# Decoder block on one core: the first attention group's score and maxima units in a new order, its maxima row sent by ScalarE, and two group loads issued at other places

## The reference, cut to what matters

```python
Q = (x @ Wq.T + bq).reshape(b, s, H, hd)      # K, V alike
scores = (gt * scores_cross + (1.0 - gt) * scores_conv) * hd ** -0.5
scores = jnp.where(causal, scores, -jnp.inf)
attn = jax.nn.softmax(scores, axis=-1)
out = jnp.einsum('bhqk,bkhd->bqhd', attn, V)
```

## Time and profile before

| | before |
|---|---|
| median of 3 runs | 1066.88 us |
| the runs | 1066.5, 1066.88, 1082.13 us |
| the profiled execution, its own time | 1068.4 us |
| its span, first to last instruction | 1066.7 us |
| mean granted TensorE clock | 0.985 of full |
| PE busy | 1024.2 us |
| DVE busy | 720.5 us |
| ACT busy | 576.9 us |

### The profile page before, as it was taken

The page is one execution under the profiler, slowest core; times in us unless marked ns, Lnnn a source line. Parts: engine busy times, 40 slices in busy tenths (PEclk is TensorE's granted clock), DMA queues, the critical chain, the costliest instruction groups (busy, mean ns, idle before and its releaser), DMA issues.

```text
span 1066.7 us, 19123 instructions
## 1 busy us (share of the span) xinstructions
PE 1024.2 (96%) x7108; PEld 604.0 (57%) x7108; DVE 720.5 (68%) x1603; ACT 576.9 (54%) x1093; POOL 198.3 (19%) x220
## 2 busy tenths in 40 slices
PE   4999899999999999999999999899999999999998
PEld 3877344444444444444444465444544588888887
DVE  6878887877787787878785386556566355555552
ACT  3776276767676676767676667376466411111110
POOL 6655000000000000000000034111001033333331
PEclk9999799999999999999999999899999999999999
DMA  8596904444433344444401046688663100000001
GB/s 259 189 269 222 192 2 81 82 82 82 82 62 57 65 72 81 86 85 82 81 13 20 11 122 159 141 157 155 124 118 62 31 8 21 20 21 20 20 21 40
DMA packets 82186, 93.27 MB, mean 87 GB/s; under 512 B 14660, under 2 KB 75296, under 8 KB 80557
## 3 DMA queue, kind: packets, MB, share of 16 engines
q1 hardware_dynamic: 79579, 88.87, 38.2%
q10 hardware_dynamic: 2514, 3.18, 1.4%
HBM read 53.55 MB, written 28.80 MB: 77 GB/s over the span
## 4 chain that ended last, share of the span: by engine, by line
PE 78%; DVE 12%; ACT 3%; issue 2%; DMA 2%; SPq 1%; POOL 0%; POOLq 0%; DVEq 0%; ACTq 0%
PE bank L134 20%; PE bank L837 12%; PE bank L870 12%; PE bank L856 10%; DVE pm L767 5%; PE bank L1503 3%; PE bank L1128 3%; PE bank L860 3%; PE bank L842 2%; PE bank L1395 2%; PE bank L1405 2%; PE bank L968 2%; PE bank L1397 2%; PE bank L1380 2%; PE bank L1382 1%
## 5 line engine op out<-in xcount | busy, mean ns | idle before, releaser
L767 DVE TENSOR_REDUCE pm<-bank 128x1 f32<-128x512 f32 (+3 forms) x608 | 356.5, 652 | 86.4 <-PE bank L842 69.7
L814 ACT ACTIVATE prob<-bank 128x512 f32<-128x512 f32 (+1 forms) x608 | 317.4, 584 | 172.0 <-PE bank L860 86.8
L837 PE MATMUL bank<-stk,stq 96*128 96x512 bf16 (+3 forms) x768 | 223.5, 334 | 5.5 <-DVE pm L767 3.4
L856 PE MATMUL bank<-stq,stk 98*128 98x512 bf16 (+3 forms) x768 | 221.0, 328 | 1.7 <-DMA stq<-mrow 0.8
L837 PEld LDWEIGHTS bank<-stk,stq 96*128 96x128 bf16 x768 | 67.9, 97 | 134.2 <-DVE pm L767 76.9
L870 PE MATMUL bank<-prob,va 128*17 128x512 f32 (+3 forms) x1536 | 143.8, 492 | 0.0
L1630 ACT ACTIVATE e_sg<-bank 128x512 f32<-128x512 f32 x48 | 28.7, 598 | 177.0 <-PE bank L134 174.9
L1349 ACT ACTIVATE xprob<-bank 80x512 f32<-80x512 f32 x128 | 72.8, 593 | 71.7 <-PE bank L1397 68.8
L753 POOL TENSOR_TENSOR xres<-xres,bo_b 128x256 f32<-128x256 f32 x32 | 23.2, 724 | 398.5 <-DVE pm L767 204.1
L856 PEld LDWEIGHTS bank<-stq,stk 98*128 98x128 bf16 x768 | 69.1, 98 | 45.4 <-ACT prob L814 9.1
L842 PE MATMUL bank<-tri_q,identb 128*128 128x128 bf16 (+2 forms) x352 | 87.0, 247 | 0.0
(11 more groups left out here) (183 smaller groups left out, 1347.1 us busy)
## 6 DMA issues: line engine op xcount, KB each, us to landing
qk<-a_parts SPq DMA_DIRECT2D x32, 384.0 KB, 2.7
xq<-c_parts SPq DMA_DIRECT2D x16, 384.0 KB, 3.1
xstq<-xq SPq DMA_DIRECT2D x32, 192.0 KB, 4.3
stq<-qk SPq DMA_DIRECT2D x30, 192.0 KB, 3.9
stk<-qk SPq DMA_DIRECT2D x15, 384.0 KB, 6.3
vs<-a_vst SPq DMA_DIRECT2D x8, 544.0 KB, 3.8
oall<-u_out SPq DMA_DIRECT2D x64, 64.0 KB
xstq<-xq SPq DMA_DIRECT2D x32, 128.0 KB, 4.7
```

The source lines that it names most:

```text
L767: nc.vector.tensor_reduce(pm[:, k, h0:h0 + hb, r], src[:, 0:hb * w].rearrange("p (h w) -> p h w", h=hb), AX, ALU.max).then_inc(s_mxe, 1)
L814: nc.scalar.activation(prob[:, U % NPS, 0:hb * n], bank[STB[U % NSB]][:, 0:hb * n], ACT.Exp).then_inc(s_ex, 1)
L837: mm = nc.tensor.matmul(dst[:, h * w:(h + 1) * w], stq[i][0:R, half, h0 + h, r * P:(r + 1) * P], stk[i][0:R, h0 + h, k0:k0 + w], start=(h ...
L856: mm = nc.tensor.matmul(dst[:, h * n:(h + 1) * n], stk[i][0:RM, h0 + h, kt * P:(kt + 1) * P], stq[i][0:RM, half, h0 + h, q0:q0 + n], start ...
```

## The change

- Group 0 gets an order of its own (`first_plan`). Ahead of the barrier TensorE does ring places 11 to 15 only (`LEAD` = 16) instead of 11 to 38. After it come places 16 to 19, then the first half's 11 score units with the other 19 places among them (one or two with each), then, behind unit 10, the second half's transpose and the first 6 maxima units of group 1, and then the 27 score units of the second half with the other 33 maxima units of group 1 among them. The other groups keep `plan`. VectorE's code doesn't change its order, but `self_vector(v, range(N_AHEAD, NMX - 1))` stays as it is: it goes through places 11 to 38 as they come, and waits for the barrier after them.
- ACT arrives at the barrier, then waits for the first half's row of group 0 and sends it (`send_maxima(a, 0, 0)`), then waits for the barrier. SP sent it before, after the barrier.
- SP issues group 1's load behind chunk 5's stores, ahead of those of chunks 6 and 7.
- SP issues group 2's load, behind group 0's second maxima row. ACT did so before.

```diff
--- before.py
+++ after.py
@@ -271,7 +271,8 @@
 
             for c in range(NCH):
                 chunk(c)
-            load_self(sp, 1)
+                if c == 5:
+                    load_self(sp, 1)
             for u in range(2):
                 sp.wait_ge(so[u], 64 * B)
                 sp.wait_ge(vo[u], 16 * B)
@@ -659,6 +660,29 @@
             plan += [("r", n, 1) for n in range(at, upto)]
             at = upto
 
+        LEAD = n_half + 5
+
+        def first_plan():
+
+
+            own = [("r", n, 0) for n in range(LEAD, NMX - 1)]
+            order, own = own[:4], own[4:]
+            ahead = [("r", n, 1) for n in range(NMX - 1)]
+            for u in range(NST):
+                order.append(("s", u, 0))
+                order += [("p", s, 0) for s in range(len(sets)) if joint_end[s] - 1 == u - LAG]
+                if u < half_end[0]:
+                    upto = len(own) * (u + 1) // half_end[0] - len(own) * u // half_end[0]
+                    at = len(own) * u // half_end[0]
+                    order += own[at:at + upto]
+                if u == half_end[0] - 1:
+                    order += [("r", NMX - 1, 0)] + ahead[:6]
+                    ahead = ahead[6:]
+                if u >= half_end[0]:
+                    w, n = u - half_end[0], NST - half_end[0]
+                    order += ahead[len(ahead) * w // n:len(ahead) * (w + 1) // n]
+            return order
+
         side[0] = "right"
         stq, stk, va = [], [], []
 
@@ -710,11 +734,14 @@
                               .rearrange("c (r h) s -> (c r) h s", h=HP)[:, heads]).then_inc(ld[n], 16)
             eng.dma_start(va[n][:].rearrange("p n d h -> p n (d h)"), vs[g]).then_inc(ld[n], 16)
 
+        def send_maxima(eng, g, c):
+            eng.wait_ge(s_mxe, g * NMX + ring.index(("t", c)) + 1)
+            eng.dma_start(stq[g % NB][R:RM, c].rearrange("a h q -> a (h q)"),
+                          mrow[:, g % 2, c]).then_inc(md[g % 2][c], 16)
+
         def self_sync(sp):
             def maxima(g, c):
-                sp.wait_ge(s_mxe, g * NMX + ring.index(("t", c)) + 1)
-                sp.dma_start(stq[g % NB][R:RM, c].rearrange("a h q -> a (h q)"),
-                             mrow[:, g % 2, c]).then_inc(md[g % 2][c], 16)
+                send_maxima(sp, g, c)
 
             def store(g):
 
@@ -728,9 +755,11 @@
                 sp.dma_start(den[rows * i:rows * (i + 1), b],
                              u_out[HD:P:VW, g % 2].rearrange("a (c t) -> a c t", t=DT)).then_inc(us[g % 2], 16)
 
-            maxima(0, 0)
             for g in range(G):
                 maxima(g, 1)
+                if g == 0:
+                    for i in range(2, NB):
+                        load_self(sp, i)
                 if g:
                     store(g - 1)
                     if g + NB - 1 < G:
@@ -804,8 +833,6 @@
                 nc.scalar.activation(u_out[:, g % 2, c * 512:(c + 1) * 512], bank[PVB[c]][:],
                                      ACT.Identity).then_inc(s_u, 1)
 
-            for i in range(2, NB):
-                load_self(a, i)
             for g in range(G):
                 for u, (half, kt, h0, hb, q0, n, diag) in enumerate(st_units):
                     U = g * NST + u
@@ -880,7 +907,7 @@
             t.wait_ge(s_r, 4 * NCH)
             t.wait_ge(s_ve, 2 * NCH)
             for g in range(G):
-                for what, which, ahead in plan:
+                for what, which, ahead in plan if g else first_plan():
                     if g == G - 1 and what == "s" and which in EARLY:
                         if which == min(EARLY):
                             t.wait_ge(s_mxe, G * NMX)
@@ -1829,7 +1856,9 @@
             @block.scalar
             def _(a):
                 qkv_scalar(a)
-                barrier(a, 1)
+                arrive(a)
+                send_maxima(a, 0, 0)
+                a.wait_ge(s_phase, 5)
                 self_scalar(a)
                 mid_scalar(a)
                 barrier(a, 2)
@@ -1841,7 +1870,7 @@
             def _(t):
                 qkv_tensor(t)
                 arrive(t)
-                self_tensor(t, range(N_AHEAD, NMX - 1))
+                self_tensor(t, range(N_AHEAD, LEAD))
                 t.wait_ge(s_phase, 5)
                 self_tensor(t, None)
                 mid_tensor(t)
```

## The result

The changed kernel's median is 1073.59 us over 20 runs, that of the kernel before 1068.55 us over 20, runs that are added to the three shown above. The ratio is 1.0062, with a 95% interval of 1.0042 to 1.0082: 4.5 to 8.8 us slower, within 2%. The ratio leaves out executions over 1.5% above the fastest of their kernel; the two medians alone lie 5.0 us apart. The forecast was 1068.9 us, 2.0 us slower than before, with a range up to 1072.2.

A forecast was written before the change was run, and what follows sets the result against it. It took TensorE to bound the kernel and VectorE's reductions to pace the passage between the stages. +1.4 (to the second half) and +0.6 (second half) made +2.0 on 1066.9, so 1068.9 us; range 1065.3 to 1072.2.

The forecast's parts named there:

- What bounds the passage: From 109 us until group 0 is through: scores beside maxima help only as far as VectorE does not stop.
- VectorE's slack: From 109 us to group 1's first score: 38 us of reductions in 45.6 us, some 7 us of slack.
- When the barrier opens: End of stage one: last value store lands after 6.2 us behind the moved load, barrier opens at 115.2, as today.
- faster: Rival at the barrier: store lands at 112.3, barrier opens at 112.4; total 1065.9 us, chance 17%.
- VectorE's stop: Behind the first transpose, at the barrier: VectorE loses 4.8 us, eight reductions, from 111.6 to 116.4.
- To the second half's first score: From the barrier to that score: VectorE sets the pace, score at 134.5 against 133.09, +1.4 us.
- VectorE's starving: In group 0's 23 reductions behind the barrier: 0.7 us, bounds 0.3 and 1.6; over 1.6 means the prediction is wrong.
- The row: Second half's maxima row by DMA: flight of 2.7 us in place of 6.53, with no load under way.
- The late row: Rival at the second half's row: flight stays 6.53 us in place of 2.7, +3.8, 1072.7 us; chance 8%.
- The second half: From its first score to group 1's: two more maxima units there, priced nearer TensorE's 0.6 than VectorE's 1.2; +0.6 us.
- second fall: Rival around the second transpose: TensorE's clock falls to half again, +1.5 us, 1070.4; chance 25%.
- intended gain: Rival between the stages: TensorE's 9.5 us of waits vanish, 1058 us; large gain and unknown losses together 5%.

The follow-up runs named there:

- the two other places of the load: Changed kernel with group 1's load behind the last chunk (1077.05 us, ratio to before 1.0063) or right behind the barrier (1073.88 us, 1.0056).
- The halved reductions: Changed kernel with VectorE's reductions for group 1's maxima reading half their columns, exponentials scaled by 0.01; ratio 1.0047.
- the second profile of the changed kernel: Changed kernel profiled once more, nothing edited; group 1's first score 52.99 us behind the last value store's issue, against 50.32 in its first profile.
- The second pair: Kernel before and changed kernel, each profiled once more unedited; group 1's first score at 47.43 and 52.99 us behind the last value store's issue.
- 9 with an early barrier: Changed kernel with group 1's load behind the barrier and ring places 11 to 19 ahead of it; ratio 1.0008.
- five fillers ahead and one behind each unit: Kernel before with moved loads and ACT's send, plus unused matmuls: five ahead of place 14, one behind each from 15; 1066.96 us, ratio 0.9983.
- the changed kernel with fillers: Changed kernel plus 24 matmuls into an unused bank, 6 ahead of ring place 14 and 18 behind place 15; 1072.22 us, ratio 1.0043.

## Why the prediction was wrong in size, step by step

- **What bounds the passage.** Right up to the second half: the stop at the barrier is paid in full, for moving the barrier's opening by 2.4 us moved the rest by 2.45. Of the 7 us that it called VectorE's slack, though, 4.4 lay in the second half's stretch and could not be used (below). There the chain of the kernel before goes through TensorE alone (busy for 21.44 of 21.49 us); in the changed kernel 8.4 of its 23.9 us go through VectorE.
- **When the barrier opens.** Right: the store took 5.8 us to land (forecast 6.2, and 5.8 to 6.4 in all kernels with the load in front, 3.3 to 3.4 without). That the load's issue had hidden the store's landing, and that its traffic now lengthens it, is shown by the two other places of the load: 3.4 and 3.3 us to landing there, 5.8 here. The *faster* rival fell by this.
- **VectorE's stop.** Forecast 4.8 us, measured 4.42.
- **To the second half's first score.** Forecast +1.4, measured +2.25 (26.46 against 24.21). The term that was off is VectorE's starving, put at 0.7 with a bound of 1.6: the pauses are 0.45, 0.27 and 1.22, together 1.94, past the bound that the prediction had named as its sign of being wrong. I had let three full banks cover the products. The products take 1.64 us on the chain, and with unit 10's own matmuls ahead of them and the next maxima unit behind them the time without a new maxima unit exceeds three reductions by 1.2. The sum for TensorE there was also short: 9.5 for the units, 1.64 for the products and 1.7 for the low clock are 12.8 us, not 12, only half a us under VectorE's 13.3.
- **The row.** Forecast 2.7 us; at most 2.45 measured, from the copy's end at 130.84 to 133.29, and the chain goes through the reductions there, not the row. The 6.53 us of the earlier trace rows had both loads in front, and no load was under way here (DMA share 0 from 130 to 131.6 us). The late row was no danger. The fixed cost of about 2.0 us that the Trainium skill gives (DMA: Bandwidth & Descriptors, Anatomy of one DMA) is stated there for a transfer that GpSimd issues; this one is issued by SP, and the bound of 2.45 us doesn't contradict it.
- **The second half.** This is the step that failed most: forecast +0.6, measured +2.37 (23.86 against 21.49). I took TensorE's price of two more units since TensorE was busy for 21.45 and VectorE for 17.13 of 21.5 us. But four more units of group 1, not two, were unreduced at the stretch's start: 34 reductions in it against 30, 2.2 us more VectorE work (19.3 against 17.1). In both kernels VectorE is idle for 4.4 to 4.5 us of the stretch, chiefly at the products, when no maxima unit can be made. That 17.13 + 4.4 = 21.5 is true by definition; that the 4.4 us could not be used is what the changed kernel shows, where 2.2 us more work left 4.5 us idle. So VectorE had no slack there, though its busy share was 80%. The halved reductions leave at most 0.66 of the 2.37 us to TensorE, which is my +0.6; the rest is VectorE's.
- **The rivals.** The *second fall* is real, in one of two profiles of the changed kernel and two of the eight derived ones with its order, and cost 2.4 us where 1.5 was forecast. It belongs to the spread of every kernel with this order and not to one outcome; at 3 in 10 it adds 0.7 us to the mean. In the second profile of the changed kernel TensorE stood for 1.8 us, was granted 0.50 from 133.8 to 138.0 us and 1.00 again from 140. The Trainium skill (TensorE: Matmul & The Clock Gate, What's actually happening) has the clock fall behind an idle window and rise behind a busy one; the trace agrees in direction. But the prediction had it that by this rule the case comes true, and the same wait was followed by the fall in only three of ten executions. The *intended gain* could not come: the 9.5 us of waits of the earlier trace rows were TensorE's, beside a VectorE that never stopped. Two figures of the rivals don't follow from their own sums: 1066.9 - 0.8 is 1066.1 for the *faster* one, not 1065.9, and 1066.9 - 9.5 is 1057.4 for the *intended gain*, not 1058. Neither decides anything.
- **The time itself.** The sum was made on a median of three runs, 1066.88 us, and 20 give 1068.55. Of the 4.7 us between forecast and measurement, 1.7 are this and 2.6 the two terms above; the rest, under half a us, is within the spread.

What stays open: the medians' 5.0 us is close to the 4.6 of the two first profiles, but the interval, 4.5 to 8.8 us, lies mostly above it. The second pair gives 5.6 (52.99 - 47.43), and falls in three of ten would give 0.7 us more. The long stretch at half clock near 690 us doesn't seem to come more often after the change: the mean granted clock was 0.981 or less, as in the profiles with some 30 us of it (0.975 to 0.979), in 6 of 20 executions of the changed kernel and in 27 of the 73 of the kernel before that ran beside the experiments.

## What to carry to other kernels

Before units of two engines are interleaved, add up each engine's busy time from the point of change to the point that matters, and add the idle time that its partner's bursts force on it in any case; an engine that is 80% busy with the rest forced has no slack. What is left to do ahead of a barrier must keep the engine that sets the pace busy until the barrier opens: 5 places ahead lost 4.6 us, 9 with an early barrier lost none. And look at what a DMA's issue time was hiding, here the landing of the last store, before the DMA is moved.

## What the runs showed of the hardware that was not expected

- From 112.4 to 123.6 us the kernel before did maxima units alone, each when VectorE had freed a bank, and stayed at 1.2 GHz (0.50 granted) although PE is shown busy for all of the 11.2 us; the clock rose at 125.9 us, 2.2 us after the first score. With five fillers ahead and one behind each unit it was 1.00 for the whole passage.
- TensorE standing for 1.8 us behind the products (128.5 to 130.3), with short units after it, was followed by half clock from about 132.1 us in the profile of the changed kernel with fillers, from 132.6 in one of the changed kernel itself and from 131.2 in that of the halved reductions, and by none in the seven others with the new order.
- A transfer of 8 KB took 6.53 us behind two loads and at most 2.45 with the DMAs free; the value store of 544 KB took 3.3 to 3.4 us with no load ahead of it and 5.8 to 6.4 with a load of 1.8 MB issued some 19 us ahead of it.
